# First cross-attention of a decoder: the scores of the next round moved to the start of a round, and one large projection a round placed between the second and third turning

## The reference, cut to what matters

```
q = (x @ Wq.T + bq), k = (ctx @ Wk.T + bk), v = (ctx @ Wv.T + bv)      per head: 16 columns
scores = q @ k.T / 4 + bias[b]; masked to -inf
out = softmax(scores) @ v; out @ Wo.T + bo
x = layernorm(x + out)
```

## Time and profile before

| | us |
|---|---|
| median of 3 runs (lowest, highest) | 841.51 (840.01, 844.86) |
| the profiled execution | 838.83 |
| its span, first to last instruction | 837.0 |
| busy over the span: PE, PEld, DVE, ACT, POOL | 788.8, 594.6, 652.8, 610.5, 426.4 |
| first cross-attention, from the first turning of round 3 to the last weighing | 175.38 |

### The profile page before, as it was taken

How to read it: one execution, slowest core, us unless ns; L and a number is a source line. 1 busy time by engine, 2 the same in 40 slices (tenths; PEclk the granted TensorE clock), 3 DMA queues, 4 the chain that set the end, 5 groups by cost and what they waited for, 6 DMA issues and landing times.

```text
span 837.0 us, 20931 instructions
## 1 busy us (share of the span) xinstructions
PE 788.8 (94%) x6901; PEld 594.6 (71%) x6901; DVE 652.8 (78%) x2466; ACT 610.5 (73%) x1595; POOL 426.4 (51%) x459
## 2 busy tenths in 40 slices
PE   8998999999899988999999999999999999999996
PEld 7876777677667766767777777777666777676785
DVE  4997778889898767778778666785888888976667
ACT  4547977887885366887788877884999999984331
POOL 1264566666744145452554534224865666335763
PEclk9999999999999999999999999999999999999998
DMA  9301771122102458979869888875122212100001
GB/s 317 141 26 45 217 194 61 52 71 83 71 14 83 170 174 260 298 221 283 251 214 273 244 254 270 260 217 181 43 67 69 67 68 68 65 2 0 27 26 52
DMA packets 105393, 115.05 MB, mean 137 GB/s; under 512 B 29061, under 2 KB 94085, under 8 KB 105030
## 3 DMA queue, kind: packets, MB, share of 16 engines
q1 hardware_dynamic: 104724, 113.35, 42.8%
q10 hardware_dynamic: 562, 0.35, 0.1%
HBM read 48.09 MB, written 51.82 MB: 119 GB/s over the span
## 4 chain that ended last, share of the span: by engine, by line
PE 44%; ACT 7%; DVE 7%; issue 3%; DMA 3%; POOL 1%; SPq 0%; DVEq 0%; ACTq 0%
PE bank L1544 7%; PE bank L242 6%; PE bank L250 5%; PE bank L2267 4%; PE bank L2253 3%; PE bank L1559 3%; PE bank L2284 3%; PE bank L1528 2%; PE bank L1585 2%; PE bank L1595 2%; PE bank L2319 2%; ACT Sx L1750 2%; PE bank L234 1%; DMA skew_scratch<-rw 1%; ACT q_heads L1758 1%
## 5 line engine op out<-in xcount | busy, mean ns | idle before, releaser
L242 PE MATMUL bank<-x_feat,w_all_mats 128*128 128x256 f32 x384 | 92.4, 385 | 2.2 <-ACT q_full L358 0.6
L2997 POOL TENSOR_TENSOR bnd<-bnd,consts 128x60 f32<-128x60 f32 x64 | 18.1, 304 | 137.2 <-DMA bnd<-band_scratch 137.2
L242 PEld LDWEIGHTS bank<-x_feat,w_all_mats 128*128 128x128 f32 x384 | 70.4, 191 | 14.7 <-ACT rw L2644 3.8
L2602 ACT ACTIVATE bias_area<-bias_area,mq_two 128x256 f32<-128x256 f32 x128 | 66.5, 534 | 0.0
L1003 DVE COPY q_heads<-bank 128x512 f32<-128x512 f32 x64 | 42.0, 685 | 23.4 <-PE bank L717 23.3
L2778 DVE COPY q_heads<-bank 128x512 f32<-128x512 f32 x64 | 41.1, 683 | 22.8 <-PE bank L2267 22.8
L896 ACT ACTIVATE Sx<-Sx,mq 128x256 f32<-128x256 f32 x128 | 54.4, 497 | 5.4 <-DVE mq L995 5.4
L904 ACT ACTIVATE q_heads<-bank 128x512 f32<-128x512 f32 x64 | 37.7, 589 | 26.4 <-PE bank L717 26.4
L1750 ACT ACTIVATE Sx<-Sx,mq 128x256 f32<-128x256 f32 x128 | 54.3, 501 | 2.3 <-DVE mq L1848 2.3
L1856 DVE COPY q_heads<-bank 128x512 f32<-128x512 f32 x64 | 42.1, 685 | 17.0 <-PE bank L1544 17.0
L896 ACT ACTIVATE Pr<-Pr,mq 128x256 f32<-128x256 f32 x128 | 54.3, 501 | 0.9 <-DVE mq L995 0.9
(11 more groups left out here) (309 smaller groups left out, 2340.3 us busy)
## 6 DMA issues: line engine op xcount, KB each, us to landing
dist<-skew_scratch SPq DMA_DIRECT2D x64, 296.0 KB, 4.1
skew_scratch<-rw SPq DMA_DIRECT2D x30, 588.0 KB, 4.4
bnd<-band_scratch SPq DMA_DIRECT2D x64, 108.0 KB, 2.7
band_scratch<-bias_area SPq DMA_DIRECT2D x32, 162.0 KB, 3.2
band_scratch<-bias_area SPq DMA_DIRECT2D x32, 148.0 KB, 2.6
skew_scratch<-dist SPq DMA_DIRECT2D x4, 1024.0 KB, 7.7
context_values<-dist SPq DMA_DIRECT2D x8, 512.0 KB, 2.6
v_two<-context_values SPq DMA_DIRECT2D x8, 512.0 KB, 4.2
```

Of the source, the lines that this page charges most:

```text
L242: last = pe.matmul(dst[:, m * S:(m + 1) * S], w[:, k, m * P:(m + 1) * P], rhs[:, k, :], start=(k == 0), stop=(k == FT - 1))
L2602: last = act.activation(rows_of(n, g)[:, t, :], rows_of(n, g)[:, t, :], ACT.Exp, bias=mq_two[:, n % 2, g, t:t + 1], scale=-1.0, accum_out= ...
```

## The change

On TensorE, from round 4 on (in batch 0 from the second round on), scores(n + 1) moves from behind turn(n, 1) to the start of round n, right behind weigh(n - 2) of the round before. The large work of `m_bank` is placed so that V, K and Y stand between turn(n, 1) and turn(n, 2) of the first, second and fourth round; Q stays behind turn(n, 3) of the third. VectorE's and ScalarE's side work moves with it: `copy_v` and the residual add now stand in the middle of the eight reductions of the second and first round, the norm's statistics, `fold_peak`, both `normalise` and `fold_statistics` between the eighth reduction and the first copy.

More of the change, by code:

```diff
@@ L818, in third_round @@
                         weigh(n - 1)
+                    def fourth_round(b, n):
+                        if b < B - 1:
+                            scores(n + 1)
+                        turn(n, 0)
+                        turn(n, 1)
                         if b >= 1:
@@ L955, in _ @@
                             exps(n, 0)
-                            exps(n, 1)
-                            if j == 1 and b < B - 2:
-                                copy_k(b + 2 if b else 1)
-                            if n == 2:
-                                copy_k(2)
                             if j == 3 and b < B - 2:
                                 copy_q(b + 2)
+                            exps(n, 1)
+                            if n == 1:
+                                copy_k(1)
                             if n >= 1:
@@ L970, in _ @@
                                 copy_ot(n - 2)
+                            if j == 1 and b < B - 2:
+                                copy_k(b + 2)
                             if j == 2 and b >= 1:
@@ L1182, in _ @@
-                            if j == 0 and b >= 2:
-                                norm_begin(dve, y_steps, b - 2, y_mm, b - 1, m_bank, True, parts=(1,))
-                            peaks(n, 3)
-                            if j == 0 and b >= 2:
-                                norm_begin(dve, y_steps, b - 2, y_mm, b - 1, m_bank, True, parts=(2,))
-                            if n == 0:
-                                gru_norm_end(dve, B - 1)
-                            if j == 0:
-                                copy_v(b)
@@ L1198, in _ @@
                             turned(n, 1)
-                            if j == 2 and b >= 2:
-                                fold_statistics(b - 2)
-                            if j == 0 and b >= 3:
-                                fold_peak(b - 3)
-                    norm_begin(dve, y_steps, B - 2, y_mm, B - 1, m_bank, True, parts=(1, 2))
+                    dve.wait_ge(biased, B - 1)
+                    dve.wait_ge(kept, B - 2)
+                    norm_begin(dve, y_steps, B - 2, y_mm, B - 1, m_bank, True)
```

20 lines of the change are left out of this document (8 added, 12 removed).

## The result

| | before | after |
|---|---|---|
| median of 20 runs each (lowest, highest), us | 840.55 (838.68, 844.86) | 843.69 (841.97, 847.77) |
| the profiled execution, its span | 838.83, 837.0 | 846.16, 844.3 |
| granted TensorE clock over the span | 0.997 | 0.993 |

A forecast was written before the change was run, and what follows sets the result against it. Heavy batches were taken as bound by a loop through TensorE and VectorE, light ones by VectorE. Terms -1.9 + 2.6 - 0.2 + 0.7 = +1.2 us on the median 841.51 gave 842.7, range 837.5 to 848.5.

The forecast's parts named there:

- The loop: First turning through VectorE's copies and reductions to the next scores sets the intervals; batches 2 to 5 gain 1.9 us.
- The bare loop: Same cycle with nothing standing among the reductions: 0.69 + 1.20 + 2.75 + 0.14 + 0.68 = 5.46 us.
- Light batches: Batches 6 and 7, without K and Q to fill TensorE: together 51.9 us against 49.34, +2.6.
- Batch 0: First batch, scores waiting for reductions, turnings for copies, and partly for batch 1's k: +0.7 us.
- a partial wait for k's transfer (0.3): In the first batch, scores at 86.43 wait for batch 1's k to land: 0.3 us taken of 0 to 0.5.
- 2.6 turnings that wait for copies: TensorE-bound interval of the first batch: 1.08 + 2.6 + 1.73 + 1.00 = 6.41 us, 2.6 being the turnings.
- Behind the stage: After the last weighing, batch 6's norm and the last `fold_statistics` come later but are covered: costed at 0.
- the bound of 1.2: Cost after the stage if nothing covers the later work: the norm's statistics, 1.2 us.
- The cover named: TensorE's context projections and VectorE's weight statistics after the stage, claimed to hide the later work, leaving 0.
- Rival 1: Faster: scores hardly wait in heavy batches, intervals about 5.4; 11.2 us faster, 830.3; chance 0.2, including part of it.
- Rival 2: Slower: each of some 28 loop passages costs 0.15 us more, +4.2 on top of 1.2, 847; chance 0.25.
- Rival 3: GpSimd late, K's transfer or bias slipping past fourth-round scores: +4 us per us of slip, 846.7; chance under 0.05.

The follow-up runs named there:

- Experiment 8: Kernel with the changed order in batches 1 to 5 only, with `copy_v` moved behind the eighth reduction: 836.85 us, ratio 0.9955 to the kernel before.
- Experiment 6: Changed kernel with batches 6 and 7 put back in the order of before: 841.87 us, ratio 1.0020 to the kernel before.
- Experiment 4: Changed kernel with `copy_k(2)` of batch 0 put back in the third round: 842.32 us, ratio 1.0037 to the kernel before.
- experiment 5: Changed kernel with batch 0 alone put back in the order of before: 841.76 us, ratio 1.0014 to the kernel before.
- experiment 10: Changed kernel with only the last batch's `fold_statistics` put back in the third round: 844.46 us, ratio 1.0044 to the kernel before.
- experiment 2: Kernel before with Y moved into the fourth round, residual add and norm statistics behind the next first round's eighth reduction, in all batches: 838.89 us, ratio 0.9984.
- experiment 3: Changed kernel with `copy_v`, residual add and its statistics moved behind the eighth reduction: 842.86 us, ratio 1.0034 to the kernel before.

## Why the prediction came out right, and where it was off

- **The loop.** Right in mechanism and size. Forecast intervals 6.18, 6.06, 6.50, 6.20; measured 6.14, 6.11, 6.51, 6.28. Batches 2 to 5 gave 1.64 of 1.9 expected. The bare loop, 5.46, stands in the light batches as forecast. Experiment 8 takes one term of 0.60 out of the loop and gets 0.57 in that interval, of which the next one gives back 0.16.
- **Light batches.** Right: 51.96 for 51.9, and batch 6 from first turning to first turning 23.83 (212.71 to 236.54) for 23.85. Experiment 6 undoes them.
- **Batch 0.** Mis-sized: +1.89 for +0.7. The step costed TensorE's pieces and a partial wait for k's transfer (0.3). It did not follow `copy_k(2)`, which the change moves a round forward, to its own wait on GpSimd's split. The term that was too small is "2.6 turnings that wait for copies", for which the prediction shows no row: the two pairs of turnings occupy 3.97 (from 80.88, when the scores of 79.80 are through, to Q at 84.85). The 0.3 for k's transfer was not needed; it had landed. Experiment 4 shows that taking the wait of `copy_k(2)` away gives back only 0.33, since the transfer then takes over as a wait of 0.65; experiment 5, that both vanish with the old order.
- **Behind the stage.** Mis-sized: +1.02 for 0, inside the bound of 1.2 but by another mechanism than that bound's. The cover named (context projections, weight statistics) did not hide GpSimd's late affine fold, because that fold slows VectorE by 1.11 and 0.96 in two operations while the weight statistics are awaited, and TensorE then stands 0.76 for them. Experiments 6 and 10 both bring the tail back to 21.3.
- **Rival 1** (TensorE's waits vanish) is refuted by the waits of 0.53 to 1.03 before the scores, and by intervals of 6.14 and 6.11 where it needed about 5.4. **Rival 2** (0.15 more per passage): the measured intervals leave under 0.1 a passage. **Rival 3**: GpSimd did get late, but it struck in the tail, not at the fourth round's scores.
- **The total.** +1.2 was forecast and some 3.4 measured; the two mis-sized terms are most of the difference (1.2 and 1.0 too little). In absolute time, 842.7 for 843.69 looks closer than that by luck: it was built on a median of three runs, 841.51, and that of twenty is 840.55. On that base the forecast is 841.75.
- The misses share a direction. Where a term was costed at nothing or nearly so, the thing moved had a wait or a neighbour on a third engine that was not followed up.

## What to carry to other kernels

When an order is changed for all batches, read each kind of batch apart: experiment 2 was a loss of 2.2 us in the light batches and a gain of 2.8 in the heavy ones, in one number that said "no change", and a condition on the batch made it a gain. Cut the stretches so that the same work lies in both, or the moved piece itself is counted as gain and loss: here it made -4.8 and +4.2 of them. When work is moved behind the end of a loop to fill a gap, add up all that then stands in the gap: 1.2 us in 1.5 was worth 2.1 us over five batches; 2.8 us in the same 1.5, of which GpSimd made 0.9, was worth almost nothing. For each operation moved forward, look up what its own buffer waits for, on every engine.

## What the runs showed of the hardware

Two kinds of VectorE's operations stretch while a GpSimd product over 128x512 runs: a `tensor_scalar` on two columns 0.17 to 1.28 (and 1.07 in experiment 3), a 128x512 product with both inputs in SBUF 0.69 to 1.65. L216 ends 0.02 and 0.03 behind GpSimd's instruction (265.48 and 265.46; 144.37 and 144.34), the product 0.57 behind it (267.65 and 267.08), which is most of its own 0.69. Operations that read a bank kept their times next to the same GpSimd work: in experiment 3 the add L201 took 0.69 inside a GpSimd product that ran from 141.15 to 142.43. So did the norm's statistics, which read SBUF alone (L207, 0.41 to 0.43 each with or without such a product beside them, in after). And once it was GpSimd that was late: its pass at 265.53 took 1.55, before 1.28, with VectorE's L1121 (0.40, before 0.41) lying inside it from 265.56.
